# Two of four waves of SBUF-to-SBUF DMAs moved from SyncE's queue to ScalarE's in an attention and feed-forward kernel

## The reference

```
x = x + sum over heads h of  softmax(causal(q_h k_h^T / sqrt(128))) v_h W_O[h]^T,   q, k, v from LN(x)
x = x + LN'(x) ternary(W)^T + bias          (LN' with gamma and beta)
```

## Time and profile before

| what | value |
|---|---|
| runs, median (lowest to highest) | 810.5 us (810.34 to 811.31), 3 runs |
| the profiled execution, own time | 810.04 us |
| its span | 808.2 us |
| granted TensorE clock, mean | 0.999 |
| PE busy | 799.1 us, 99% |
| DVE busy | 674.2 us, 83% |
| ACT busy | 557.7 us, 69% |
| POOL busy | 550.8 us, 68% |
| DMA queue q1 | 57168 packets, 110.56 MB, 57.1% of 16 engines |

### The profile page before, as it was taken

How to read it: one execution, slowest core, us unless ns; L and a number is a source line. 1 busy time by engine, 2 the same in 40 slices (tenths; PEclk the granted TensorE clock), 3 DMA queues, 4 the chain that set the end, 5 groups by cost and what they waited for, 6 DMA issues and landing times.

```text
span 808.2 us, 14644 instructions
## 1 busy us (share of the span) xinstructions
PE 799.1 (99%) x4844; PEld 722.8 (89%) x4844; DVE 674.2 (83%) x1471; ACT 557.7 (69%) x1031; POOL 550.8 (68%) x282
## 2 busy tenths in 40 slices
PE   8999999999999999999999999999999999999997
PEld 7898999898899898899999899999899989899896
DVE  8987887887888888788888788788878788888998
ACT  6976766667676667766677777667676666677674
POOL 6278865696676956778557776568666685577585
PEclk9999999999999999999999999999999999999999
DMA  6466666555666556666555666655666655566503
GB/s 190 97 146 150 155 161 141 123 130 140 168 143 147 124 137 151 147 145 151 139 138 125 157 154 160 143 118 130 145 168 143 139 132 118 137 147 141 131 1 105
DMA packets 57242, 111.49 MB, mean 138 GB/s; under 512 B 16976, under 2 KB 21200, under 8 KB 57168
## 3 DMA queue, kind: packets, MB, share of 16 engines
q1 hardware_dynamic: 57168, 110.56, 57.1%
HBM read 10.88 MB, written 2.10 MB: 16 GB/s over the span
## 4 chain that ended last, share of the span: by engine, by line
PE 95%; DVE 2%; DMA 1%; ACT 1%; issue 0%; SPq 0%; DVEq 0%
PE scores L731 24%; PE ring L684 24%; PE ring L664 22%; PE ring L694 11%; PE ring L673 11%; PE ring L653 1%; PE scores L721 1%; PE ring L628 1%; DMA acc<-in_x 1%; DVE acc L981 0%; DVE turn L896 0%; DVE stats L926 0%; DVE xT L961 0%; ACT turn L822 0%; DVE scores L888 0%
## 5 line engine op out<-in xcount | busy, mean ns | idle before, releaser
L550 POOL TENSOR_TENSOR pT<-pT 128x1024 fp32r<-128x1024 f32 x186 | 447.2, 2408 | 224.6 <-ACT pT L829 221.8
L829 ACT ACTIVATE pT<-pT 128x1024 fp32r<-128x1024 f32 x186 | 197.4, 1062 | 173.9 <-DMA pT<-turn 173.8
L888 DVE CUSTOM_DVE_ANT_0 scores<-scores,mask 128x128 f32<-128x128 f32 (+7 forms) x256 | 194.7, 762 | 71.3 <-PE scores L731 69.6
L731 PE MATMUL scores<-kT,qT 128*128 128x512 f32 (+2 forms) x1056 | 228.9, 350 | 0.0
L896 DVE STREAM_TRANSPOSE turn<-turn 128x128 f32<-128x128 f32 (+1 forms) x248 | 184.8, 764 | 50.3 <-ACT turn L822 49.8
L822 ACT ACTIVATE turn<-scores,negmax 128x128 f32<-128x128 f32 (+7 forms) x256 | 188.0, 735 | 47.4 <-DVE negmax L888 46.4
L684 PEld LDWEIGHTS ring<-pT,v 128*128 128x128 f32 x1116 | 189.8, 189 | 26.4
L684 PE MATMUL ring<-pT,v 128*128 128x512 f32 x1116 | 209.4, 341 | 0.0
L731 PEld LDWEIGHTS scores<-kT,qT 128*128 128x128 f32 x1056 | 173.9, 189 | 17.5
L694 PE MATMUL ring<-wo_s,zT 128*128 128x256 f32 x768 | 112.8, 283 | 0.5 <-DVE zT L959 0.5
L908 DVE SCALAR_TENSOR_TENSOR acc<-ring,inv,acc 128x256 f32<-128x256 f32 x256 | 108.9, 467 | 0.1
(11 more groups left out here) (86 smaller groups left out, 549.4 us busy)
## 6 DMA issues: line engine op xcount, KB each, us to landing
pT<-turn SPq DMA_DIRECT2D x496, 128.0 KB, 2.3
pT<-turn SPq DMA_DIRECT2D x496, 64.0 KB, 2.0
acc<-in_x SPq DMA_DIRECT2D x8, 256.0 KB, 5.1
wk_raw<-in_wk SPq DMA_DIRECT2D x8, 256.0 KB, 3.4
wq_raw<-in_wq SPq DMA_DIRECT2D x8, 256.0 KB, 2.9
wv_raw<-in_wv SPq DMA_DIRECT2D x8, 256.0 KB, 3.0
norm<-in_wo SPq DMA_DIRECT2D x8, 256.0 KB, 3.1
out<-acc SPq DMA_DIRECT2D x7, 256.0 KB, 2.2
```

The costliest lines, as they stand in the source:

```text
L550: pool.tensor_tensor(chunk(half, LO, c), f32(chunk(half, LO, c)), f32(chunk(half, HI, c)), ALU.subtract).then_inc(plo_ready, 1)
L731: mm = pe.matmul(scores[:, t % 2, first + c:first + c + n], qT[:, par, a, t * P:(t + 1) * P], kT[:, par, m, c:c + n], start=(i == 0), stop ...
L829: act.activation(chunk(half, HI, c), f32(chunk(half, LO, c)), ACT.Copy).then_inc(phi_ready, 1)
L888: dve.tensor_tensor_reduce(out=tile, in0=tile, in1=mask[:, S - (t + 1) * P:S], scale=-1.0, scalar=FAR, op0=ALU.add, op1=ALU.min, accum_out ...
```

## The change

The helper `wave` moves out of SP's block and takes the engine that issues. Waves 2 and 3 of half 0 leave SP's tables and stand in ACT's, ahead of the first copy of half 0. Waves 0 and 1 of half 0 and all of half 1 stay with SP. What each wave waits for, what it moves and the semaphore that it raises are as they were.

```diff
 SCALAR = (
     ("pv", 0, -1), ("hip", 1, 3, -1), ("exp", 4, 0), ("v", 1, 0), ("exp", 5, 0), ("qk", 3, 1), ("qk", 1, 1),
-    ("hip", 0, 0, 0), ("exp", 6, 0), ("exp", 7, 0), ("hip", 0, 1, 0), ("pv", 1, -1), ("exp", 0, 1), ("exp", 1, 1),
+    ("wave", 0, 2, 0), ("wave", 0, 3, 0), ("hip", 0, 0, 0), ("exp", 6, 0), ("exp", 7, 0), ("hip", 0, 1, 0), ("pv", 1, -1), ("exp", 0, 1), ("exp", 1, 1),
...
 SYNC = (
     ("wave", 1, 1, -1), ("wave", 1, 2, -1), ("wave", 1, 3, -1), ("wave", 0, 0, 0), ("wave", 0, 1, 0), ("load", -1),
-    ("wave", 0, 2, 0), ("wave", 0, 3, 0), ("wave", 1, 0, 0),
+    ("wave", 1, 0, 0),
...
 START_SCALAR = (
...
-    ("hip", 0, 0, 0), ("v", 0, -1), ("norm", 7), ("qk", 3, 1), ("v", 1, 0), ("qk", 2, 2), ("exp", 0, 1),
+    ("wave", 0, 2, 0), ("wave", 0, 3, 0), ("hip", 0, 0, 0), ("v", 0, -1), ("norm", 7), ("qk", 3, 1), ("v", 1, 0), ("qk", 2, 2), ("exp", 0, 1),
...
-    ("hip", 1, 3, 0), ("exp", 5, 1), ("qk", 3, 2), ("qk", 1, 2), ("exp", 6, 1), ("exp", 7, 1), ("hip", 0, 0, 1),
+    ("hip", 1, 3, 0), ("exp", 5, 1), ("qk", 3, 2), ("qk", 1, 2), ("exp", 6, 1), ("exp", 7, 1), ("wave", 0, 2, 1), ("wave", 0, 3, 1), ("hip", 0, 0, 1),
...
 START_SYNC = (
...
-    ("wave", 0, 1, 0), ("wave", 0, 2, 0), ("wave", 0, 3, 0), ("wave", 1, 0, 0), ("wave", 1, 1, 0), ("wave", 1, 2, 0),
-    ("wave", 1, 3, 0), ("next", "o", 0), ("wave", 0, 0, 1), ("wave", 0, 1, 1), ("wave", 0, 2, 1), ("wave", 0, 3, 1),
+    ("wave", 0, 1, 0), ("wave", 1, 0, 0), ("wave", 1, 1, 0), ("wave", 1, 2, 0),
+    ("wave", 1, 3, 0), ("next", "o", 0), ("wave", 0, 0, 1), ("wave", 0, 1, 1),
...
+        def wave(engine, half, a, u):
+
+            engine.wait_ge(flip_ready, u * QT + HALF * (half + 1))
+            if u > 0:
+                engine.wait_ge(job_done, job["pv", half, u - 1] + 1)
+            elif half == 1:
+                engine.wait_ge(turn_clear, 1)
+            for b in range(A):
+                engine.dma_start(f32(pT[half][b * Q:(b + 1) * Q, LO, a, :, :]),
+                                  turn[half][a * Q:(a + 1) * Q, b, :, :, :].rearrange("p j t i -> p j (t i)")
+                                  ).then_inc(wave_in[half][a], 16)
...
-                    wave(*item[1:])
+                    wave(sp, *item[1:])
...
                 if kind == "hip":
                     probs_hi(*item[1:])
+                elif kind == "wave":
+                    wave(act, *item[1:])
```

More of the change, by code:

```diff
@@ L462, in load @@
                 sp.dma_start(dst[:, :, :], src).then_inc(landed, 16)
[L464 to L474, removed]
             def next_load(which, p):
```

## The result

The changed kernel takes 866.8 us (866.2 to 867.1, 4 runs), the kernel before 810.4 beside it: the ratio is 1.0695, with a 95% interval from 1.0682 to 1.0708. The forecast was 864, range 836 to 888. The profiled execution took 867.07 us, 57.0 more than the one before. First the page of the changed kernel: busy times, the chain that ended last (by engine), and the copies of L829, the answers to the earlier trace rows.

What follows compares the result with a forecast made beforehand. PE, busy 99% of the span, was taken to bound the kernel. 810.0 us profiled + 50.7 for 28 steady steps + 3.1 at the start, the end left as it is, gave 863.8, so 864 us, range 836 to 888.

Steps and rivals of the forecast that it cites:

- The price of an issue: On ACT's queue: 0.65 us per DMA issue, SP's pace for the same DMAs; eight per unit, 5.2 us.
- below, 0, if ACT's engine goes on while its queue issues: Lower bound on the price of an ACT issue: 0; the upper bound was 2.06 us, SP's longest.
- the longer loop sets the pace: Steady units: the longer of two loops sets the step, +1.81 us per unit, 50.7 us over 28 steps.
- loop A: Through SP: exp 7, flip 7, half-1 waves, ACT's copies, eight issues, back to exp 7; 25.88 us per unit.
- loop B: Through PE: v job, qk 1, ACT's eight issues, exp 7, flip 7, DVE's take, next v job; 25.58 us per unit.
- that term, 3.62 us: From the ACT copy of the last half-1 wave to the qk copy, 3.57 us, plus handover 0.05.
- The start: Units 0 to 2: ACT's 3.2 us idle partly covers 5.2 us of issues; unit 2's half-1 waves come 3.1 us later.
- SP's wait for P·V: Sign at L468: SP's wait, 61.7 us before, moves from the P·V matmuls to the flip.
- 1, no change: ACT's issue is cheap or overlaps its engine, PE stays full: 810 to 811 us; chance 0.06.
- 4, faster: SP free earlier, PE's holes at start and end shrink: 801 to 808 us; chance 0.03.
- 2, a smaller price: Same loop, issues of 0.43 to 0.53 us or PE's stall regained elsewhere: 812 to 836 us; chance 0.06.
- 3, that issues grow dear beside SP's: SP and ACT collide or ACT's issues are slower, 0.75 us or more each: over 888 us; chance 0.07.

Runs made afterwards that it cites:

- interleaved: Kernel before, with the eight moved issues per unit on ACT singly, each behind an ACT instruction: 810.6 us; with units 0 and 1 so too, 810.0 us.
- one wave: Changed kernel with wave 2 of half 0 back on SP, only wave 3 on ACT, start tables of before: 811.9 us, ratio 1.0014 to before.
- three waves: Changed kernel with wave 1 of half 0 on ACT too, 12 DMAs per unit, start tables of before: 963.2 us, ratio 1.1885 to before.
- split: Changed kernel with wave 2 ahead of hip 0 0 and wave 3 behind exp 7, start tables of before: 813.3 us, ratio 1.0044 to before.
- stand-ins: Kernel before, all DMAs on SP, with 27, 41 or 55 one-column ACT copies ahead of hip 0 0: 810.7, 836.7 and 877.2 us.
- late: Changed kernel with both moved waves behind exp 7, start tables of before: 951.7 us, ratio 1.1765 to before.
- 55 copies: Kernel before, all DMAs on SP, with 55 one-column ACT copies per unit ahead of hip 0 0: 877.2 us, ratio 1.0810 to before.

## Why the prediction was right, and where it was not

**What bounds the kernel** was read rightly. SP's queue looked full and was not the bound; relieving it is worth nothing (interleaved kernels). The Trainium skill's advice to balance DMAs over engines (Perfetto Trace Analysis, "DMA Optimizations") is given for a kernel whose bottleneck is the issue; this one's is PE, and the move pays nothing: 809.96 against 810.12 us at best.

**The price of an issue**, 0.65 us taken from SP's rows, holds on ACT: median 0.612 us, and eight of them with the handover 5.11 us at least, 5.39 in the mean. The bound "below, 0, if ACT's engine goes on while its queue issues" was half true in a way that I had not seen: the engine does go on, but only with what stands ahead of the issues. Singly and spread over the queue, they cost nothing (interleaved; 0.52 us each in the median); in a row of eight each costs its full time. The Trainium skill's "usually small relative to the DMA itself" (DMA: Bandwidth & Descriptors) is true of one issue here, 0.61 of the 2.0 us that ACT's DMAs take to land; what decides is the row of eight.

**The loops.** That the pace is set by a loop through exp 6, exp 7 and ACT's queue is shown by one wave, three waves, split and the stand-ins, and the waits of PE are the ones named. The forecast time held, but one step of it failed: "the longer loop sets the pace", with loop A the longer. In the changed kernel the first issue comes 0.10 us after the end of PE's qk 1 in all 29 steady units, never later: what releases it is always PE, so it is loop B. Loop A was reckoned 25.88, because I let the issues wait until the qk copy had begun. They begin up to 1.2 us before it (in 15 of 29 units ahead of it), so that term, 3.62 us, is too long: in the unit shown it is 3.02 (335.21 to 338.23), which leaves at most 25.28 for loop A there. The forecast step of 25.88 against 25.73 measured is close partly by luck: it is loop B's floor of 25.44 plus 0.29, and the blocks of eight issues are 0.28 us longer in the mean than the shortest (5.39 against 5.11).

**The start** was mis-sized: 3.1 us forecast, 9.6 measured. I let 5.2 us of issues be absorbed by ACT's idle time and did not ask who waits for ACT there. Behind the issues and hip 0 0 stands a copy of v, and PE's qk job waits for its take: PE's timeline of the changed kernel has it,

```profile
35.45 1.63 PE L664 MATMUL ring<-xT,wk_s 128*128 128x512 f32 x6
40.58 2.93 PE L664 MATMUL ring<-xT,wq_s 128*128 128x512 f32 x6 [3.50 <-DVE v L961]
```

3.50 us of idle, and then six matmuls in 2.93 us in place of 1.52, since the clock is down. So the sum, 50.7 + 3.1 = 53.8 forecast, 46.9 + 9.6 + 0.5 = 57.0 measured, had one term 4 too large and one 6.5 too small.

**Signs.** As forecast: ACT's issues of some 0.6 us in groups of eight, PE's idle ahead of the score tiles and the v job, half-1 waves straight after flip 7 (347.78 to 347.81), landings no longer awaited for half 0. One was half right: SP's wait for P·V did not go but grew, from 61.7 to 224.9 us, since SP is there sooner; behind it the wait for the flip came in, 82.1 us in all where it was 28.7, and it ends last. **Rivals:** 1, no change, and 4, faster, are refuted by 866.8 us; what 1 assumes, that issues overlap ACT's engine, is true in the interleaved kernels. 2, a smaller price, is refuted by 5.11 us at least for eight, 0.64 each. 3, that issues grow dear beside SP's, is not seen (612 against 590 ns).

## What to carry to other kernels

A queue with idle time is not free to take work: follow what stands behind the new work in order, and who waits for that, until you are back where you began; if that loop is shorter than the period of the bound, the work costs nothing, and beyond that it costs in full, once per round. Here DMA issues on an engine that computes did best singly, each behind an instruction of about its own length or more (0.6 to 1.1 us); the same eight issues cost 49 us in a row and nothing one by one, begun earlier. Where a change makes PE wait in every round, look at its granted clock as well: in three of these kernels (late, three waves, 55 copies) it fell behind such waits, and they took more time than their loops alone.

## What was not expected of the hardware

- **ACT's queue runs ahead of its engine.** An issue starts while instructions before it are still waiting for the engine: 338.23 against a qk copy at 338.78, and as soon as 0.10 us after the event for which that copy waits. The Trainium skill (Perfetto Trace Analysis, "DVE / Act Engine Instruction") describes a wait queue and an execution FIFO between sequencer and engine; the trace agrees, with the addition that an issue did not pass a copy whose semaphore was still to come.
- **Short ACT instructions overlap.** One-column copies last 0.19 us each but follow one another after 0.09 (55 in 5.14 us), so their durations must not be added up.
- **The half clock.** Idle times of PE of mostly 0.3 and 0.5 us per unit (the change) left the clock at 1.00 from 300 to 750 us; 3.5 us (the start), 4.6 us (late), and 2.07, 0.59 and 0.52 us within 3 us (three waves) were followed by stretches at 0.50, the 1.2 GHz level. The size of the idle time does not settle it: with 55 copies 0.51, 0.58 and 0.52 us in the unit at 293 us were followed by such a stretch, and 0.58, 0.58 and 0.53 us in the unit at 347 us were not, nor were 3.12 us in the late kernel (at 319 us). What decides is not shown. The clock has a part in the late kernel's step of 28.93 us over a floor of 26.63, and in the three-wave kernel's 29.36 over 28.39; later landings and long issues have a share in that which I did not take apart.
